# A decoder layer in one program: mixtures and sums read from SBUF, a low-rank stage by token halves, three norms on VectorE, new orders on all engines

## The reference

```
# layernorm without weights in front of each of the three parts; x is the residual
x = x + attn(layernorm(x));  x = x + xattn(layernorm(x), ctx, ctx);  x = x + ffn(layernorm(x))

def attn(x):                                   # an RWKV block
    h = layer_norm(x, ln1_w, ln1_b);  hh = time_shift(h)       # hh: the token before, 0 for the first
    xk = h * tmk + hh * (1 - tmk);    xv, xr the same with tmv, tmr
    k, v, sr = xk @ Wk.T, xv @ Wv.T, sigmoid(xr @ Wr.T)
    x = x + (sr * wkv(decay, first, k, v)) @ Wo.T              # wkv: a recurrence over the tokens
    h = layer_norm(x, ln2_w, ln2_b);  hh = time_shift(h)
    xk = h * fk + hh * (1 - fk);      xr = h * fr + hh * (1 - fr)
    return x + sigmoid(xr @ Wrec.T) * (square(relu(xk @ Wkey.T)) @ Wval.T)    # 1024 hidden

def xattn(q, k, v):                            # inside one token: 16 heads of 16 numbers,
    s = q_heads . k_heads / 4, head i sees heads 0..i          # a 16 x 16 causal table per token
    return softmax(s) @ v_heads

def ffn(x):                                    # rank 64
    return (gelu((x @ U1) @ V1 + b1) @ U2) @ V2 + b2
```

## Time and profile before

| | us |
|---|---|
| median of 3 runs | 1203.92 |
| their lowest and highest | 1201.18, 1204.0 |
| span of the profiled execution, first to last instruction | 1199.4 |
| TensorE busy (matmuls) | 1020.8, 85% |
| VectorE busy | 952.5, 79% |
| ScalarE busy | 940.2, 78% |
| GpSimd busy | 901.1, 75% |
| mean granted TensorE clock | 0.947 of full speed |

### The profile page before, as it was taken

One profiled execution on the slowest core, in us unless ns is written; L12 is line 12 of the kernel. 1 busy time (PEld: TensorE's weight loads), 2 busy tenths in 40 slices (PEclk: granted clock), 3 DMA queues, 4 the chain that ended last, 5 costly groups with the idle time before them and its releaser, 6 DMA issues.

```text
span 1199.4 us, 14602 instructions
## 1 busy us (share of the span) xinstructions
PE 1020.8 (85%) x3584; PEld 586.0 (49%) x3584; DVE 952.5 (79%) x2092; ACT 940.2 (78%) x2007; POOL 901.1 (75%) x862
## 2 busy tenths in 40 slices
PE   2569698989899898989899898989898998969506
PEld 1237264654647363655646373645546473727202
DVE  3654889898989899798979898898979888757470
ACT  3778779888888979888888889888888888584504
POOL 0220997969696988969696978969696969978780
PEclk9889799999999999999999999999999999989767
DMA  5010020201111020201111110202011010201000
GB/s 176 18 23 31 1 53 1 71 0 54 18 54 19 9 62 1 72 0 53 18 53 18 33 38 1 72 0 62 9 53 36 17 37 0 54 1 36 1 17 18
DMA packets 38983, 38.54 MB, mean 32 GB/s; under 512 B 2932, under 2 KB 38648, under 8 KB 38904
## 3 DMA queue, kind: packets, MB, share of 16 engines
q1 hardware_dynamic: 30456, 29.38, 7.4%
q0 software_dynamic: 8448, 8.39, 4.6%
HBM read 29.38 MB, written 8.39 MB: 31 GB/s over the span
## 4 chain that ended last, share of the span: by engine, by line
PE 46%; ACT 25%; DVE 13%; issue 7%; POOL 6%; SPq 1%; DMA 0%; ACTq 0%; POOLq 0%; DVEq 0%
PE bank L832 18%; PE bank L889 12%; PE bank L920 5%; ACT n L480 4%; PE bank L839 4%; DVE bank L1345 4%; POOL prod L329 3%; ACT shift L473 3%; ACT q L480 3%; PE bank L913 3%; PE bank L932 2%; POOL prod L350 2%; DVE stat L1154 2%; ACT hidden L598 1%; ACT rr L546 1%
## 5 line engine op out<-in xcount | busy, mean ns | idle before, releaser
L329 POOL TENSOR_TENSOR prod<-q,kv_ctx 128x256 f32<-128x256 f32 (+5 forms) x448 | 360.1, 853 | 140.6 <-ACT q L480 140.6
L350 POOL TENSOR_TENSOR prod<-prob,v_dh 128x256 f32<-128x256 f32 (+3 forms) x256 | 383.9, 1606 | 0.0
L832 PE MATMUL bank<-xk,w_key 128*128 128x512 f32 x512 | 233.4, 605 | 11.3 <-DVE xk L1196 11.3
L889 PE MATMUL bank<-w_val,hidden 128*128 128x256 f32 x1024 | 225.9, 379 | 0.0
L1345 DVE TENSOR_REDUCE bank<-prod 128x64 f32<-128x256 f32 (+3 forms) x256 | 192.0, 819 | 34.8 <-POOL prod L350 25.4
L889 PEld LDWEIGHTS bank<-w_val,hidden 128*128 128x128 f32 x1024 | 193.5, 190 | 31.7 <-issue 6.7
L1318 DVE TENSOR_REDUCE score<-prod 128x16 f32<-128x256 f32 (+5 forms) x448 | 177.1, 466 | 19.5 <-POOL prod L329 19.4
L832 PEld LDWEIGHTS bank<-xk,w_key 128*128 128x128 f32 x512 | 97.7, 193 | 127.7 <-issue 111.0
L846 PE MATMUL bank<-ident,n 128*128 128x128 f32 x384 | 66.2, 302 | 103.4 <-ACT n L480 101.0
L565 ACT ACTIVATE hidden<-bank 128x512 f32<-128x512 f32 x128 | 74.1, 593 | 82.8 <-PE bank L832 82.7
L846 PEld LDWEIGHTS bank<-ident,n 128*128 128x128 f32 x384 | 49.3, 155 | 159.6 <-issue 153.7
(11 more groups left out here) (95 smaller groups left out, 1909.9 us busy)
## 6 DMA issues: line engine op xcount, KB each, us to landing
x_in<-in_x SPq DMA_DIRECT2D x16, 512.0 KB, 3.5
x<-in_x POOLq DMA_DIRECT2D x16, 512.0 KB, 5.7
kv_ctx<-in_ctx SPq DMA_DIRECT2D x16, 512.0 KB, 4.5
out<-y_out SPq DMA_DIRECT2D x16, 512.0 KB, 3.2
w_key<-in_wkey SPq DMA_DIRECT2D x1, 1024.0 KB
w_val<-in_wval SPq DMA_DIRECT2D x1, 1024.0 KB
w_k<-in_wk SPq DMA_DIRECT2D x1, 256.0 KB, 3.6
w_v<-in_wv SPq DMA_DIRECT2D x1, 256.0 KB, 4.4
```

What stands on the lines that cost most here:

```text
L329: ins = pool.tensor_tensor(o, a, b, ALU.mult)
L350: ins = pool.tensor_tensor(o, ph[:, HB * n:HB * n + HB, 0:keys].unsqueeze(2).to_broadcast(shape), vh[:, :, 0:keys].unsqueeze(1).to_broadca ...
L832: mm = pe.matmul(to[:, :], w[:, fi, P * f:P * f + P], src[:, fi, :], start=(fi == 0), stop=(fi == CH - 1))
L889: mm = pe.matmul(bank[6 + t // 2][:, C * (t % 2):C * (t % 2) + C], hidden[:, j, P * t:P * t + P], w_val[:, j, :], start=(j == 0), stop=(j ...
```

## The change

- `h1` and `h2` are new SBUF tensors of 257 columns a sequence, the first of them 0. ScalarE writes the norm with its weights there once (`affine_1`, `affine_2`), each present share is then one ScalarE instruction from SBUF to SBUF (`own_share`), and `add_before` reads `h` (SBUF) one column earlier and the mixture (SBUF).
- `sum_values` writes to `o_sum` in SBUF; `over_mass` and `third_residual` read it there.
- Norms 2, 3 and 4 are applied on VectorE, `(x - mean) * rstd` as `tensor_scalar`, with no `shift`; norm 1 stays on ScalarE, its `shift` made by one VectorE instruction.
- The low-rank stage holds tokens 0 to 255 in the upper 64 rows and 256 to 511 in the lower ones. `project_u1`, `project_v1`, `project_u2` and `project_v2` work on pairs of tiles of 256 columns, `pT` and `qT` have 256 columns, one `gelu` reads two banks.
- The last residual is written over `x3`, and the output is stored from there one step later; `y_out` is gone, and `n4` shares the place of `n2`. The value projection is cut in pieces between the last key projections. PSUM banks are dealt out anew, the pipeline has one step more at its end, the loop covers steps 6 to 13 where it covered 5 to 14, and the order of all engines is new.

```diff
             def add_before(dst, f, src, name):
-                m = MIXES.index(name)
-                x = src[:, :].rearrange("p (s t) -> p s t", s=SEQ)
-                out = seqs(dst, f)[:, :, 1:T]
-                return dve.scalar_tensor_tensor(out=out, in0=x[:, :, 0:T - 1], scalar=prev_w[:, m, f:f + 1],
+                at = VECS.index(name) * CH + f
+                out = seqs(dst, f)
+                return dve.scalar_tensor_tensor(out=out, in0=before(src, f), scalar=other[:, at:at + 1],
                                                 in1=out, op0=ALU.mult, op1=ALU.add)
...
+            def normalise(n, g, dst, src, done):
+                dve.wait_ge(rstd_done[n], upto(g, 1))
+                for t in range(TT):
+                    ins = dve.tensor_scalar(dst[:, t, :], src[:, t, :], mv[n][:, t, 0:1], rstd[n][:, t:t + 1],
+                                            ALU.subtract, ALU.mult)
+                ins.then_inc(done, 1)
...
+            def shift_1(g):
...
+                dve.scalar_tensor_tensor(out=shift[:, :], in0=mv[1][:, :, 0], scalar=-1.0,
+                                         in1=rstd[1][:, :], op0=ALU.mult, op1=ALU.mult)
+                dve.tensor_tensor(ln_ratio[:, :], lnc[:, :], lnv[1][:, :], ALU.subtract).then_inc(shift_ready[1], 1)
...
-                    ins = dve.tensor_reduce(bank[5][:, row:row + HB * HD], src, AX.X, ALU.add)
+                    ins = dve.tensor_reduce(o_sum[:, row:row + HB * HD], src, AX.X, ALU.add)
...
-                o = bank[5][:, :].rearrange("p (h d) -> p h d", d=HD)
+                o = o_sum[:, :].rearrange("p (h d) -> p h d", d=HD)
...
-                dve.tensor_tensor(pair(x3[par], s), bank[5][:, :], pair(x2[par], s), ALU.add).then_inc(x3_done, 1)
+                dve.tensor_tensor(pair(x3[par], s), o_sum[:, :], pair(x2[par], s), ALU.add).then_inc(x3_done, 1)
...
-                act.activation(out[:, :, 0:1], x[:, :, 0:1], ACT.Identity,
-                               bias=first_b[:, m, f:f + 1], scale=w)
-                return act.activation(out[:, :, 1:T], x[:, :, 1:T], ACT.Identity,
-                                      bias=col(norm + "_b", f), scale=w)
+                act.activation(now(h1, f), by_seq(TR1_BANK[f]), ACT.Identity,
+                               bias=col("ln1_b", f), scale=col("ln1_w", f)).then_inc(h1_done, 1)
+            def own_share(dst, f, src, name):
+                return act.activation(seqs(dst, f), now(src, f), ACT.Identity, scale=col(name, f))
...
             def project_u1(g):
                 pe.wait_ge(n4T_done, upto(g, 2))
                 for fi in range(CH):
-                    mm = pe.matmul(bank[3][:, :], w_u1[:, fi, :], n4T[:, fi, :],
-                                   start=(fi == 0), stop=(fi == CH - 1))
+                    for e in range(2):
+                        mm = pe.matmul(bank[U1_BANK][RANK * e:RANK * e + RANK, 0:W // 2], w_u1[:, fi, :],
+                                       n4T[:, fi, W // 2 * e:W // 2 * e + W // 2],
+                                       start=(fi == 0), stop=(fi == CH - 1))
...
+                for t in range(2):
+                    for e in range(2):
+                        rows = slice(RANK * e, RANK * e + RANK)
+                        mm = pe.matmul(bank[Y_BANK[e]][:, C * t:C * t + C], qT[rows, P * t:P * t + P],
+                                       w_v2[rows, :], start=False, stop=(t == 1))
```

1294 lines of the change are left out of this document (785 added, 509 removed).

## The result

| | before | after |
|---|---|---|
| median, us (4 runs each, same chip) | 1202.55 | 1374.51 |
| lowest and highest | 1200.25, 1204.0 | 1368.48, 1387.31 |
| ratio to before | | 1.145, 95% interval 1.139 to 1.151 |
| span of the profiled execution | 1199.4 | 1376.8 |
| mean granted TensorE clock | 0.947 | 0.888 |

The forecast was slower (0.69), 1303 us, between 1170 and 1400. The sign and the range held. The size did not: the profiled span grew by 177 us where the sum said 100. (The profiled execution of the changed kernel took 1379.9 us, 5.4 above the median.)

What follows compares the result with a forecast made beforehand. TensorE was taken to bound the 66.5 us step before, VectorE after: 63.2 plus waits, taken as 75. 13 steps gave +110, the ends -10: span 1299, median about 1303 us, range 1170 to 1400.

Steps and rivals of the forecast that it cites:

- The disputed cost: VectorE instructions with SBUF-only inputs beside a working GpSimd, 28 a step: taken to wait for GpSimd, 13.3 us a step.
- The hint: GpSimd's two-tensor sum takes 1197 ns, VectorE's with one PSUM input 690 to 740, so GpSimd's SBUF path is full.
- ScalarE: Three norms and the tiny shift instructions leave ScalarE: from 58.1 to about 48 us a step, not the bound.
- TensorE: Half the columns in u1 and v2, -2.1 us: from 61.6 to 59.5 us a step, to 63.7 if weight loads show.
- VectorE's plain work: Norms add 3.6 us and shift 0.3 on VectorE: from 59.3 to 63.2 us a step, passing TensorE without any wait.
- The waits: 24 of 28 VectorE instructions wait at 0.55 us beside scores, 0.8 beside other scores and values: 13.3 us a step.
- the bound: Upper end of one VectorE wait: GpSimd's instruction under way plus its next one, at most 2.4 us.
- Fill and drain: Shorter norm chains at both ends of the pipeline: -10 us together, with +0 for waits there.
- GpSimd: GpSimd, held up in turn by 24 VectorE instructions (about 12 us), comes to 68 us a step, below VectorE.
- No wait: Rival: VectorE does not wait beside GpSimd; step 64 to 65.5 us, time about 1171 us, chance 0.27.
- The wait, but small: Rival: VectorE waits only 0.15 us apiece beside GpSimd; step 66.8 us, time 1195 to 1210 us, chance 0.04.
- the interlock: Rival: VectorE's last instruction of a step waits for ScalarE, widening TensorE's gaps; step 68.5 us, time 1220 us, chance 0.07.

Runs made afterwards that it cites:

- lock_alone: Separate kernel computing nothing of the reference: one VectorE instruction arrives during back-to-back GpSimd products; with two SBUF inputs it took at most 2706 ns.
- add_x_early: Changed kernel with GpSimd's DMA issue moved ahead of the last score products, where GpSimd stands a moment later: 1268.4 us, ratio 1.055.
- no_products: Changed kernel with GpSimd's 44 product instructions a step cut to one column each: 1107.7 us (one run), a step of 63.7.

## Why the prediction was right, and where its size failed

**The mechanism.** Right. The disputed cost was that of instructions "of a kind that the trace never shows beside a working GpSimd"; it was taken as a wait for the GpSimd instruction under way, and `lock_alone` shows that wait and nothing else: 0.55 us after the end, at every arrival, none with an input in PSUM. The hint that decided for it was the right one only in its direction. That "its way to SBUF is full while it runs" no run shows; what they show is that VectorE doesn't share, it stands to the end of GpSimd's instruction. And it is owed to the width of the range, not to the sum, that the time fell inside it: of the 172 us that were lost, 106 come from a wait that the sum didn't have. The direction didn't need that wait, since `add_x_early` without it is slower too, 1268 us.

**ScalarE.** 58.1 to 48 us a step was forecast, 48.1 came.

**TensorE.** 59.5 us of work at full clock; `no_products` has 59.8 at a granted clock of 1.00. In the changed kernel it is 65.8 at 0.90, so some of the time at 1.2 GHz, with 16.5 us of gaps in a step of 82.3. The forecast's work over that clock, 59.5 / 0.9 = 66, fits. It stays under VectorE's 82 and costs only chains. By groups, beside the earlier trace rows:

```profile
L985 PE MATMUL psum<-pT,w_v 64*128 64x256 f32 x512 | 76.9, 436 | 14.0 <-ACT pT L610 10.4 <-DVE num L1501 3.6
...
L974 PE MATMUL psum<-n4T,w_u 128*64 128x256 f32 x128 | 26.2, 550 | 3.1 <-ACT n4T L604 3.1
L1007 PE MATMUL psum<-w_v,qT 64*128 64x256 f32 x128 | 18.1, 402 | 0.0
```

`v2` halved (34.2 to 18.1 us), `u2` stayed (65.2), `v1` rose from 69.2 to 76.9. `u1` fell from 36.5 to 26.2 only; at the clock of `no_products` it is 20.0, so about half, as said. `v1` is still 74.3 us there, so 5.1 of its 7.7 us come with the halves and not with the lower clock, 0.3 us a step where +4.2 had been kept in reserve for `v1` and `u2` together.

**VectorE's plain work.** 63.2 us was forecast, `no_products` has 62.4. The norms were priced at 0.3 us; the record of one is 0.40, and they overlap by some 0.08. (The 62.4 still hold about 1 us of waits beside what GpSimd had left to do: the mixtures take 135.2 us there against 118.4 at 0.74 each.)

**The waits, the term that was mis-sized.** The forecast took 28 instructions, 13.3 us a step. Measured over the run: mixtures 187.2 + 79.4 + 37.2 = 303.8 us against 160 x 0.74 = 118.4, so 185; norms 107.3 against 65.6 in `no_products`, so 42; `o_sum` 33.7 against 22.1, so 12; `x` 69.3 against 22.0 in `no_products`, so 47. Together 286 us. The thirteen held ones are 114 of it, and the remaining 172 us over 16 groups are 10.7 us a step. Counted in the ten steps between the two DMA issues above, instruction by instruction, it is **11.1 us a step beside the 8.8 of the held one, where the sum had 13.3 and, after its allowance for shared waits, kept 11.8** (75 - 63.2). `add_x_early` has 11.2 over ten steps, and no held one. So the ordinary waits were priced almost rightly. The step that failed is the bound, "each waits until the GpSimd instruction under way has ended and GpSimd's next one has had its turn ... at most 2.4 us". It took every wait for one that ends with an instruction. One of the 28 ends with the row instead, and costs 8.8 us a step: more than any other two of them, and more than the 7.3 us that separate the step of 82.3 from the forecast 75; the small misses of the other terms go the other way. `add_x_early`, which has no such row, came out at 1268 us and a step of 73.4, where the sum as written said 1303 and 75.

The trace of before held the clue. GpSimd's products start ahead of the end of the DMA issue in it (435.34 against 435.69 us), and their records overlap from there on. But nothing in that trace could show what the overlap means, since no VectorE instruction there waits for GpSimd's reads; I had read GpSimd's rows by group, not in order of time.

**Fill and drain.** -10 us was said. Taking 13 steps of 82.3 from 1376.8 leaves 307 us against 1199.4 - 864.8 = 335, so -28. (By the DMA issues twelve steps are that long, the thirteenth is 73.0, so 9 of these 28 us are the short last step.) With the steps: 13 x (82.3 - 75) = +95, -18 for the ends, +77 together: the whole distance from 1299 to 1376.8.

**GpSimd.** 68 us a step was said, 62.2 came. That it is held up less because it keeps VectorE out in the row would fit, but no run separates this.

**The rivals.** "No wait" describes the step without GpSimd's products (64 to 65.5 us said, 63.7 measured), though not the time (1171 said, 1107.7 measured). "The wait, but small" and the interlock had no part. What I had not named at all is that a wait of VectorE can be tied to GpSimd standing still: behind the held mixture stands `sum_values`, for which GpSimd then stands. That knot is what ends the wait here.

## What to carry to other kernels

Count each VectorE instruction with two SBUF inputs (or a `tensor_scalar` from SBUF to SBUF) that runs beside GpSimd reads as a wait to the end of GpSimd's instruction, and look at what GpSimd did before: behind a DMA issue of its own the wait ran to the end of the row, mostly 9 to 20 us here, and late in a long row without a stand it could last 3 to 9 us, not always to the end. Keep one of the two inputs in PSUM (0.74 us at every arrival), and put GpSimd's DMA issue where GpSimd stands right after it; moving two lines gave 106 of 172 us back. None of the versions here beats the kernel before (1203 us): the best of the changed kernel were 1261 and 1268 us, and the kernel before with `o_sum` in SBUF and the landing wait took 1253.
